# Cross-attention kernel: value tile one block later, mask transposes apart from the sums, first weight tiles split in SBUF, last group summed by TensorE, last output tiles in four banks

## What is computed

```python
Q = split_heads(x @ Wq.T + bq); K = split_heads(ctx @ Wk.T + bk); V = split_heads(ctx @ Wv.T + bv)
scores = einsum('bhqd,bhkd->bhqk', Q, K) / sqrt(32)
scores = where(mask == 0, -1e9, scores)
out = einsum('bhqk,bhkd->bhqd', softmax(scores), V) @ Wo.T + bo
y = out + x
return (y - mean(y)) / sqrt(var(y) + 1e-5) * ln_g + ln_b
```

## Time and profile before

| what | value |
|---|---|
| median of three runs | 1893.29 us |
| the profiled execution | 1894.68 us |
| its span (first to last instruction) | 1891.7 us |
| mean granted TensorE clock | 0.976 |
| PE, PEld busy | 94%, 47% |
| DVE, ACT, POOL busy | 60%, 71%, 69% |
| DMA, mean | 87 GB/s |

### The profile page before, as it was taken

How to read it: one execution, slowest core, us unless ns; L and a number is a source line. 1 busy time by engine, 2 the same in 40 slices (tenths; PEclk the granted TensorE clock), 3 DMA queues, 4 the chain that set the end, 5 groups by cost and what they waited for, 6 DMA issues and landing times.

```text
span 1891.7 us, 34346 instructions
## 1 busy us (share of the span) xinstructions
PE 1768.8 (94%) x12816; PEld 879.7 (47%) x12816; DVE 1126.2 (60%) x2826; ACT 1345.3 (71%) x1537; POOL 1302.4 (69%) x844
## 2 busy tenths in 40 slices
PE   3889999999999999999999999999999999999984
PEld 2535445454544545454454545445454544545431
DVE  2546665656666665666666565666656566665612
ACT  2277786777878677787867778786777878677660
POOL 2074686877778687777868777786877778686574
PEclk9979999999999999999999999999999999999967
DMA  9222232232223223222322322232222223222010
GB/s 317 78 69 70 79 108 75 85 103 75 81 90 108 75 85 103 75 82 89 108 74 85 102 75 85 85 108 75 85 102 75 86 85 108 75 63 80 8 35 33
DMA packets 94020, 164.50 MB, mean 87 GB/s; under 512 B 25888, under 2 KB 34080, under 8 KB 93856
## 3 DMA queue, kind: packets, MB, share of 16 engines
q1 hardware_dynamic: 93856, 162.31, 26.4%
HBM read 140.25 MB, written 22.02 MB: 86 GB/s over the span
## 4 chain that ended last, share of the span: by engine, by line
PE 63%; ACT 11%; POOL 11%; issue 7%; DVE 5%; SPq 1%; DMA 1%; POOLq 0%; ACTq 0%; DVEq 0%
PE proj_bank L772 34%; PE ring L684 16%; POOL total L351 7%; PE ctx_bank L717 6%; ACT probs L445 5%; PE ring L726 4%; DVE ring L543 3%; ACT exp_banks L421 3%; POOL total L359 2%; PE exp_banks L702 2%; ACT q L465 2%; POOL x_lo L338 1%; PE exp_banks L693 1%; SPq L242 1%; ACT c_hi L481 1%
## 5 line engine op out<-in xcount | busy, mean ns | idle before, releaser
L543 DVE CUSTOM_DVE_ANT_0 ring<-ring,bias 128x512 f32<-128x512 f32 x1024 | 688.1, 714 | 457.4 <-PE ring L684 456.3
L445 ACT ACTIVATE probs<-exp_banks 128x1024 f32<-128x1024 f32 x512 | 523.0, 1022 | 227.5 <-PE exp_banks L702 227.5
L421 ACT CAST exp_banks<-biasT 128x1024 f32<-128x1024 bf16 x512 | 520.6, 1017 | 23.2
L684 PE MATMUL ring<-k,q 32*128 32x512 f32 x3072 | 498.2, 427 | 23.8 <-ACT exp_banks L421 13.1
L693 PE MATMUL exp_banks<-q,k 32*128 32x512 f32 x3072 | 501.6, 431 | 5.4 <-ACT exp_banks L421 5.4
L684 PEld LDWEIGHTS ring<-k,q 32*128 32x128 f32 x3072 | 251.1, 184 | 284.3 <-DVE maxes L543 149.7
L351 POOL TENSOR_TENSOR total<-probs 128x2048 f32<-128x2048 f32 x64 | 293.1, 4580 | 82.6 <-ACT probs L445 82.6
L351 POOL TENSOR_TENSOR total<-total,probs 128x2048 f32<-128x2048 f32 x64 | 293.6, 4587 | 81.2 <-ACT probs L445 79.0
L359 POOL TENSOR_TENSOR total<-total,probs 128x1024 f32<-128x1024 f32 x128 | 304.0, 2397 | 11.2 <-ACT probs L445 4.2
L717 PE MATMUL ctx_bank<-probs,v 128*32 128x512 f32 x2048 | 282.3, 624 | 0.9 <-DVE ctxT L598 0.8
L772 PE MATMUL proj_bank<-wo,ctxT 128*128 128x512 f32 x512 | 254.7, 621 | 8.4 <-DVE rows L564 4.5
(11 more groups left out here) (69 smaller groups left out, 2061.7 us busy)
## 6 DMA issues: line engine op xcount, KB each, us to landing
w_tile<-w_scratch SPq DMA_DIRECT2D x128, 512.0 KB, 3.6
raw<-cT_dram SPq DMA_DIRECT2D x64, 256.0 KB, 4.7
raw<-xT_dram SPq DMA_DIRECT2D x64, 256.0 KB, 4.5
raw<-mask_dram SPq DMA_DIRECT2D x64, 256.0 KB, 2.8
rows<-x_dram SPq DMA_DIRECT2D x64, 256.0 KB, 3.2
out_dram<-rows SPq DMA_DIRECT2D x64, 256.0 KB, 2.1
w_scratch<-k SPq DMA_DIRECT2D x8, 256.0 KB, 6.0
max_rows<-max_scratch SPq DMA_DIRECT2D x128, 8.0 KB
```

The source lines that it names most:

```text
L421: nc.scalar.copy(exp_banks[:, 2 - 2 * wave:4 - 2 * wave, :], biasT[:, kc:kc + 1, :].to_broadcast([P, 2, L])).then_inc(seeded, 1)
L445: nc.scalar.activation(probs[:, u % PS, 2 - 2 * wave:4 - 2 * wave, :], exp_banks[:, 2 - 2 * wave:4 - 2 * wave, :], ACT.Exp).then_inc(exps, 1)
L543: nc.vector.tensor_tensor_reduce(out=ring[:, n % 2], in0=ring[:, n % 2], in1=bias[:, c], scale=1.0, scalar=LOWEST, op0=ALU.subtract, op1=A ...
L684: mm = nc.tensor.matmul(ring[:, (n + h % 2) % 2], q[rows_h, g % QS, a, c * P:(c + 1) * P], k[rows_h, g % KS, b, :], start=part == 0, stop= ...
```

## The change

The plan and SP's program:

```diff
-END = UNITS + 20
-KS, QS, PS, CS, RAW = 4, 3, 4, 6, 8
+END = UNITS + 2
+LAST = GROUPS - 1
+KS, QS, PS, CS, RAW, WS = 4, 3, 4, 6, 8, 3
...
-            12: ("V", 1, 1), 13: ("K", 1, 2), 14: ("V", 1, 2), 15: ("Q", 1, 2)}
+            12: ("K", 1, 2), 13: ("V", 1, 1), 14: ("V", 1, 2), 15: ("Q", 1, 2)}
+    MASKS = {13: 0, 14: 1, 15: 2, 1: 3}
...
-        s, kc = divmod(y + 3, UPS)
-        return ("M", s, kc) if kc < NC and 0 <= s < NB else None
+        s, kc = (y + 3) // UPS, self.MASKS.get(y % UPS)
+        return ("M", s, kc) if kc is not None and 0 <= s < NB else None
...
-            for w, dst, done in ((WkT, probs[:, 0], wk_loaded), (WvT, probs[:, 2], wv_loaded),
-                                 (WqT, probs[:, 1], wq_loaded), (WoT, wo[:, :, :], wo_loaded)):
+            def load_weight(w, dst, done):
                 sp.dma_start(dst, w.rearrange("(t p) n -> p t n", p=P)).then_inc(done, FULL)
...
-            def scratch(w, parts, count, done):
-                sp.wait_ge(w_split, count)
-                for n in range(NG):
-                    for part in range(2):
-                        sp.dma_start(w_scratch[w * NG + n, :, part],
-                                     parts[part][:, :, n * P:(n + 1) * P].bitcast(FP32)).then_inc(
-                            done, FULL)
+            def scratch(w, parts, split, done):
+                sp.wait_ge(split, 2)
+                for part in range(2):
+                    sp.dma_start(w_scratch[w * NG:(w + 1) * NG, :, part].rearrange("n p t c -> p n (t c)"),
+                                 parts[part]).then_inc(done, FULL)
...
-                if i >= 2:
-                    sp.wait_ge(proj_done, PLAN.no[PLAN.qk_list[i - 2]] + 1)
+                if i >= WS:
+                    sp.wait_ge(proj_done, PLAN.no[PLAN.qk_list[i - WS]] + 1)
                 else:
-                    sp.wait_ge(wk_scratch if tile[0] == "K" else wq_scratch, 2 * NG * FULL)
+                    return
+                sp.wait_ge(wk_scratch if tile[0] == "K" else wq_scratch, 2 * FULL)
                 w = (0 if tile[0] == "K" else NG) + tile[2]
-                sp.dma_start(w_tile[:, i % 2].bitcast(FP32), w_scratch[w]).then_inc(
-                    w_loaded[i % 2], FULL)
+                sp.dma_start(w_tile[:, i % WS].bitcast(FP32), w_scratch[w]).then_inc(
+                    w_loaded[i % WS], FULL)
...
+            load_weight(WkT, probs[:, 0], wk_loaded)
             for t in range(NK):
                 load_raw(0, 0, t)
+            load_weight(WqT, probs[:, 1], wq_loaded)
             for t in range(NK):
                 load_raw(0, 1, t)
-            scratch(0, (k[:, 0:2].rearrange("p a b n -> p (a b) n"),
-                        k[:, 2:4].rearrange("p a b n -> p (a b) n")), 2, wk_scratch)
-            scratch(1, (x_hi, x_lo), 5, wq_scratch)
+            for dst, src in ((bk_s, bk), (bq_s, bq)):
+                sp.dma_start(dst[:, :], src).then_inc(qk_bias_loaded, FULL)
+            load_weight(WvT, probs[:, 2], wv_loaded)
+            load_weight(WoT, wo[:, :, :], wo_loaded)
+            for dst, src in ((bv_s, bv), (bo_all, bo), (g_all, ln_g), (b_all, ln_b)):
+                sp.dma_start(dst[:, :], src).then_inc(consts_loaded, FULL)
...
+                if y == -8:
+                    scratch(1, (total[:, :, :], rows[:, :, :]), wq_split, wq_scratch)
+                if y == -7:
+                    scratch(0, (ctxT[:, 0:NG], probs[:, 3]), wk_split, wk_scratch)
...
+                if y == UNITS - 2:
+                    for n in range(NC - 1):
+                        load_row(("O", NB - 1, n))
+            load_row(("O", NB - 1, NC - 1))
+            for n in range(NC):
+                store_row(("O", NB - 1, n))
...
```

POOL's program:

```diff
-                if k in (1, 2) and 0 <= g < GROUPS:
+                if k in (1, 2) and 0 <= g < LAST:
...
+            for n in range(NC):
+                m = PLAN.o["O", NB - 1, n]
+                pool.wait_ge(bo_ready, 1)
+                pool.wait_ge(rows_loaded[n], FULL * (m // NC + 1))
+                nc.gpsimd.tensor_tensor(rows[:, n], rows[:, n], bo_all[:, :],
+                                        ALU.add).then_inc(tail_biased, 1)
+            for n in range(NC):
+                inverse_deviation(("O", NB - 1, n))
```

ACT's program:

```diff
-            act.wait_ge(consts_loaded, 6 * FULL)
-            act.wait_ge(bq_scaled, 1)
             act.wait_ge(consts_made, 6)
-            act.wait_ge(bv_wo, 2)
...
```

DVE's program:

```diff
+            def first_tile(n, src):
+                nc.vector.tensor_copy(w_tile[:, n, 0], src).then_inc(first_hi, 1)
+                dve.wait_ge(first_hi, n + 1)
+                nc.vector.tensor_tensor(w_tile[:, n, 1], src, w_tile[:, n, 0].bitcast(FP32),
+                                        ALU.subtract).then_inc(first_lo, 1)
...
             dve.wait_ge(wk_loaded, FULL)
...
+            first_tile(0, wk_raw[:, :, 0])
             dve.wait_ge(wq_loaded, FULL)
...
+            first_tile(1, wq_raw[:, :, 0])
+            first_tile(2, wk_raw[:, :, 1])
+            dve.wait_ge(qk_bias_loaded, 2 * FULL)
...
+            dve.wait_ge(wv_loaded, FULL)
+            split(probs[:, 2], wv_hi[:, :, :], wv_lo[:, :, :], wv_split)
+            def prologue(y):
+                if y == -7:
+                    split(wq_raw, by_tile(total[:, :, :]), by_tile(rows[:, :, :]), wq_split)
+                if y == -6:
+                    split(wk_raw, by_tile(ctxT[:, 0:NG]), by_tile(probs[:, 3]), wk_split)
+                    dve.wait_ge(consts_loaded, 4 * FULL)
...
-                g, at = divmod(y - 5, NC)
-                summed = g if at == 0 and 0 <= g < GROUPS else None
+                prologue(y)
...
-                if summed is not None:
-                    widen_recip(summed)
-                    normalise_ctx(summed)
...
                     turn_sums(PLAN.sums(y)[1])
                     invert_sums(PLAN.sums(y)[1])
+                    widen_recip(PLAN.sums(y)[1])
+                    normalise_ctx(PLAN.sums(y)[1])
...
+            def finish_last(n):
+                tile, m = ("O", NB - 1, n), PLAN.o["O", NB - 1, n]
+                dve.wait_ge(tail_done, n + 1)
+                dve.wait_ge(tail_biased, n + 1)
+                nc.vector.tensor_tensor(rows[:, n], exp_banks[:, n], rows[:, n],
+                                        ALU.add).then_inc(o_out, 1)
+                row_statistics(tile)
+                row_aggregate(tile)
+            def scale_last(n):
+                m = PLAN.o["O", NB - 1, n]
+                dve.wait_ge(row_normed, m + 1)
+                nc.vector.tensor_tensor(rows[:, n], rows[:, n], g_all[:, :],
+                                        ALU.mult).then_inc(row_scaled, 1)
+                dve.wait_ge(row_scaled, m + 1)
+                nc.vector.tensor_tensor(rows[:, n], rows[:, n], b_all[:, :],
+                                        ALU.add).then_inc(row_done, 1)
+            for n in range(NC):
+                finish_last(n)
+                if n:
+                    scale_last(n - 1)
+            scale_last(NC - 1)
```

PE's program:

```diff
-            pe.wait_ge(wo_loaded, FULL)
-            pe.wait_ge(bv_wide, 1)
-            for t in range(NK):
-                mm = nc.tensor.matmul(proj_bank[:, 0], recipT[:, t], wo[:, t], start=t == 0,
-                                      stop=t == NK - 1)
-            mm.then_inc(bv_wo, 1)
-            for b in range(HG):
-                mm = nc.tensor.matmul(exp_banks[:, b], wo[:, 0, 0:P], wo[:, 0], start=True, stop=True)
-            mm.then_inc(bv_wo, 1)
-            pe.wait_ge(bo_ready, 1)
             pe.wait_ge(consts_made, 8)
-            pe.wait_ge(w_split, 7)
+            def prologue(y):
+                if y == -6:
+                    pe.wait_ge(wv_split, 2)
+                    for b in range(HG):
+                        mm = nc.tensor.matmul(exp_banks[:, b], wv_hi[:, 0, 0:P], wv_hi[:, 0],
+                                              start=True, stop=True)
+                    mm.then_inc(banks_written, 1)
+                if y == -5:
+                    pe.wait_ge(wo_loaded, FULL)
+                    pe.wait_ge(bv_wide, 1)
+                    for t in range(NK):
+                        mm = nc.tensor.matmul(ctx_bank[:, 0], recipT[:, t], wo[:, t], start=t == 0,
+                                              stop=t == NK - 1)
+                    mm.then_inc(bv_wo, 1)
...
+            def sum_last(u):
+                n = PLAN.ring["S", LAST]
+                if u % NC == 0:
+                    pe.wait_ge(ring_free, n - 1)
+                for h in range(HG):
+                    mm = nc.tensor.matmul(ring[h * D:(h + 1) * D, n % 2], ones[:, :],
+                                          probs[:, u % PS, h], start=u % NC == 0,
+                                          stop=u % NC == NC - 1)
+                if u % NC == NC - 1:
+                    mm.then_inc(ring_filled, 1)
...
+                        if i < WS:
+                            pe.wait_ge(first_lo, i + 1)
+                        else:
```

(16 more changed lines are left out.)

85 lines of the change are left out of this document (51 added, 34 removed).

## The result

| | before | after |
|---|---|---|
| median of four runs each, same chip | 1892.55 us | **1834.59 us** (1834.20 to 1835.91) |
| ratio, 95% interval | | 0.9695 (0.9678 to 0.9711) |
| span of the profiled execution | 1891.7 us | 1832.7 us |
| mean granted clock | 0.976 | 0.981 |
| PE, ACT, POOL busy | 94%, 71%, 69% | 96%, 73%, 70% |

The forecast was 1833.5 us with a span of 1832.0. The time that this document follows is the start of a block: the first score matmul of block y (of block 256, which has none, the first context matmul), from PE's list of instructions. "Tail" is what follows the start of block 256, "first value tile" the first matmul of that tile.

What follows compares the result with a forecast made beforehand. The prediction took TensorE, busy for 94% of the span, as the bound. Start 11.8, steady part 27.9 and end 20.0 summed to 59.7 us, taking the median from 1893.29 to 1833.5 us, range 1822 to 1850.

Steps and rivals of the forecast that it cites:

- First value tile, 31.5: Start: first value tile at 31.5 us instead of 47.77, 16.3 earlier, with ACT's mask conversion ahead of K's evacuation.
- mask not in the way: Start: mask lands early, K and Q wait only for POOL, Q 4.5 us sooner, 1829 in all; chance 0.08.
- The sentence on the shared port: Start: if DVE and POOL exclude each other per instruction, POOL ends at about 25.3, start 0.4 us later.
- What comes back before block 0, 4.5: Before block 0: bank-opening matmuls, DVE's Wk split and bv's matmuls return, costing 4.5 us of the start's gain.
- Value tile, 1.36 a sequence: Blocks 13 to 15: value tile one block later removes PE's idles, 1.36 us less, 15 times, 20.4 us.
- Masks, 0.47: Blocks 0 and 1: a mask moves from block 0 to 1, saving 0.47 us, 16 times, 7.5 us.
- Normalisation, nothing: Blocks with a sum: normalising ahead of DVE's next maxima makes them 0.24 us later, within 0.5 of slack, so nothing.
- the rivals on the maxima: After each sum: PE waits for DVE's maxima, partly (1848, chance 0.08) or wholly (1925, chance 0.02).
- Wait passed on: Steady part: the 1.36 us returns because another engine is next, 1854; chance 0.10, including the wait not removed.
- End, 20.0: Last group and output tiles: sum by PE and tiles without waits end the span at 1871.7, 20.0 us sooner.
- up to 2 us more: Tail: by the skill's clock rule, denser PE work frees the clock sooner, gaining up to 2 us more.
- low clock at the end: Tail: output tiles at half the clock, three of them costing 3.7 us more each, 1845; chance 0.10.

Runs made afterwards that it cites:

- s2: Changed kernel with DVE's full splits of Wv, Wq and Wk each one step later, scratch stores following: 1837.07 us, ratio 0.9689.
- s1: Changed kernel with ACT's mask conversions of the first sequence one block later, behind K's and Q's first evacuations: 1837.06 us, ratio 0.9691.
- s3: Changed kernel with both ACT's first mask conversions one block later and DVE's full splits one step later: 1831.48 us, ratio 0.9658.
- s4: Changed kernel with DVE's scaling of Wq and all behind it waiting until POOL's eight splits are done: 1833.99 us in one run.
- x1: Changed kernel with the old tile order back, value tile in block 12 and K in 13: 1851.19 us, ratio 0.9775.
- x2: Changed kernel with only the fourth mask transpose back in block 0, beside the sum: 1841.59 us, ratio 0.9724.
- x3: Changed kernel with widening and normalisation back in the block after the sum, behind its first two maxima: 1831.97 us, ratio 0.9674.
- t2: Changed kernel with the last four output tiles going through one bank in turn: 1834.89 us, ratio 0.9696.
- a1: The changed kernel unaltered, measured once more: 1834.52 us, ratio 0.9688.

## Why the prediction was right, point by point

- **First value tile, 31.5:** 32.2. The size was right for a reason that was half right. "ACT's program has the conversion of mask 0 ahead of K's evacuation" held (22.44 instead of 22.0), and s2 shows that this chain alone holds Q's projection until 25.4. But "that of Wv ends at about 20.3, before DVE is wanted at 24.2: nothing" failed: it ended at 24.7 and was as much the gate as the mask (s1, s2, s3), since the six DVE operations before it took 9.7 us beside POOL and 3.6 without it (s4). "POOL's eight splits at 4.94 us per four" failed too: 5.92 and 6.22. That the term is right to 0.7 us is luck in this: the chain that had been put at nothing came hardly later than the one that had been counted.
- **The rival "mask not in the way", 1829:** its premise that K and Q would then "wait only for POOL", 4.5 us sooner, falls; without the mask in front (s1) nothing was gained at Q's projection.
- **The sentence on the shared port:** the Trainium skill (SBUF — State Buffer, Who interferes with whom) has a VectorE operation with two SBUF inputs, or a copy, cast or tensor-scalar in a fast mode, and a GpSimd operation that reads SBUF exclude each other for a whole instruction. The trace and s4 agree: a 128x4 operation of 0.16 us took 1.23, a POOL split is some 1.23 long. The cost worked out from it was not the measured one: POOL was done at 21.1, not 25.3, and it was DVE's queue that paid.
- **What comes back before block 0, 4.5:** the first value tile came 15.6 us sooner and block 0 11.3, so 4.3. No run takes the single terms of the 4.5 apart.
- **Value tile, 1.36 a sequence:** x1 gives 1.27, blocks 13 to 15 of before and after 20.78 and 19.45, so 1.33. **Masks, 0.47:** x2 gives 0.44. Together 1.83 counted, 1.82 measured, 14 times.
- **Normalisation, nothing:** x3 gives 0.01 a sequence in sequences 1 to 14. The slack of the earlier trace rows was there; the rivals on the maxima fall. What x3's shorter sequence 15 is due to stays open.
- **Wait passed on:** no other wait came. POOL's adds were in time for block 0, as reckoned; PE waits for them in block 8 alone, 0.5 us a sequence against 0.4 before.
- **Sequence 15 was counted at a gain of 0.47 (its mask) and lost 2.5.** The granted clock there stood at 0.61 and 0.80 in the two stretches shown below. No run isolates a cause: t2 took 104.1 with the same program in it and a1 106.8, so it varies by as much from one execution to the next.
- **End, 20.0:** 22.8 (tail 24.7 instead of 27.5 as forecast). "the fourth sum follows them and takes as much": the sum was done 2.1 us after block 256 began, not 3.8, since context and sum took 1.00 and 0.86 at the high clock instead of 1.93 each. "Three more tiles without a wait, 3.71 each": 3.51. The first tile took no longer than the others, where 4.8 had been counted for it, partly at the low clock; the normalisation was covered by its first three quarters. In exchange the last tile's operations took 8.5 us, not 7.8: POOL's two operations on `rstd` (one over the deviation, 128x1) took 0.55 and 1.01 instead of 0.19 and 0.55.
- **The clock in the tail** was high: stretches of after (1752 to 1791 and 1791 to 1808 are sequence 15, 1810 to 1824 the output tiles), and the output tiles of before:

```profile
1752.00:1791.00 39.00, 31.10 (x181) 12.11 (x184) 11.52 (x30) 22.95 (x24) 28.80 (x22) 0.61 0.03 9
1791.00:1808.00 17.00, 15.02 (x104) 5.27 (x100) 2.37 (x4) 13.31 (x14) 10.29 (x9) 0.80 0.31 108
1810.00:1824.00 14.00, 14.00 (x36) 5.91 (x32) 9.61 (x17) 1.63 (x2) 4.22 (x8) 1.00 0.05 19
```

```profile
1853.00:1856.80 3.80, 3.77 (x5) 1.72 (x6) 0.00 (x0) 0.00 (x0) 0.00 (x0) 0.50 0.25 69
1857.00:1875.00 18.00, 12.67 (x28) 4.69 (x26) 7.22 (x13) 1.63 (x2) 2.02 (x6) 1.00 0.00 0
```

Before, PE had waited for the normalisation, the first output tile ran at the low clock (0.50 up to 1856.8), and from 1857 on the clock was 1.00, over the gaps between the other tiles too (PE busy for 12.67 of 18 us). After, PE went from the sum into the tiles without a wait, and all four had 1.00. The Trainium skill (TensorE: Matmul & The Clock Gate, What's actually happening) has the low clock as the default, which activity releases; the rise in before and the 1.00 over busy tiles in after agree with it. The prediction's "up to 2 us more" compares with about 3.0: 1.7 at context and sum, 1.3 at the first tile; the last tile's operations took 0.7 of it back. The rival "low clock at the end" (1845) falls.

The span came out 0.7 us above the forecast because errors cancel: 2.8 more at the end, against 0.5 less at the start and 3.1 less in the steady part (27.9 counted, 24.8 got), nearly all of it in sequence 15. Of the mechanisms, all but the single gate of the start were the right ones.
